# Quantised tiles as unsigned bytes centred by VectorE, and residual halves added ahead of the last accumulators

## The chip, the cores and the metric

The kernel runs on one core of a Trainium2 chip. The metric is the device time of one execution in microseconds (us), the median of several runs.

## The reference

`x` is (2, 512, 1024), `ctx` is (2, 1024, 1024), all float32. Four blocks follow each other, each on the layer norm of the running `x`, each added to it:

```python
def fake_quant(x, scale, zp):
    q = jnp.clip(jnp.round(x / s + z), 0.0, 255.0)
    return (q - z) * s
x = x + fake_quant(_layernorm(x)) @ fake_quant(ctx)                 # quantised product
x = x + _L0_ffn_ref(_layernorm(x), ...)     # four streams, mixed by a 50-step Sinkhorn normalisation
x = x + _L1_xattn_ref(_layernorm(x), ctx, Wq, bq, Wk, bk)           # softmax attention on ctx
x = x + _L1_ffn_ref(_layernorm(x), ...)     # out = (silu(gate) * up) @ down_w.T, each with a LoRA of rank 16
```

The change touches the first line and the very end of the last.

## The kernel before

The five engines have their own programs, written out by hand in order; semaphores join them, and each engine works strictly in its order. Tokens lie in 8 tiles of 128 rows (`g`), `ctx` in 16 tiles of 128 rows (`n`, 8 for each of the two batches).

**The front: quantisation.** SP's queue loads `x` tiles 0 to 3, context tiles 0 to 7, `x` tiles 4 to 7, context tiles 8 to 15 and then the sixteen tiles of Wq and Wk, each into the staging place `FSTAGE[n]` of a context tile once that tile has been taken (`front`, which waits on `q2_ok`). For an `x` tile VectorE forms the mean and the variance (L1532 to L1534), ScalarE a square root (L871), and VectorE the scale and the bias (`quant_rest`, L1521 to L1548). Then a tile, of `x` or of context, passes three engines:

```python
e.activation(st, st, ACT.Relu, bias=z2, scale=col(RQ2))                   # ScalarE, L887 (x: L880)
e.tensor_scalar(FSTAGE[n], FSTAGE[n], 255.0, MAGIC, ALU.min, ALU.add)     # VectorE, clip_q, L1560 (x: clip_x, L1556)
e.tensor_scalar(Q2[n // KP][:, n % KP, :], FSTAGE[n], 1.0, -(MAGIC + QHALF), ALU.mult, ALU.add)  # GpSimd, centre_q, L754 (x: centre_x, L749)
```

The division and the lower bound are ScalarE's; the upper bound and the rounding (adding 1.5 x 2^23 in float32) are VectorE's; GpSimd takes the constant off again together with 128 and writes bfloat16, on which TensorE works: it turns the `x` tile (L2506; ScalarE takes it out of PSUM, L894), sums the columns (L2525) and multiplies (L2560). VectorE adds the product to `x` (`add_product`, L1603). Between these ScalarE makes the upper halves of the weight tiles and scales the tiles (`weight_hi`, L931, L933), and GpSimd subtracts for the lower halves in four pieces a tile (`weight_lo`, L761), the last tile VectorE (L1721). TensorE's product of Wq and Wk needs all of them. Behind it run VectorE's Sinkhorn steps (L1685 to L1687) and TensorE's products (L2492 to L2494) side by side.

**The end: down projection.** A matrix product is done as seven products of blocks (names A11, A12, S1, S2, S4, S3, A22 in this order; `BLOCKS`), a scheme of Strassen's kind, and each float32 operand as two float16 halves, so three matmuls a pair (L2938). There are four output parts (`p`), each in three chunks (`j`, `SETS`) of 4, 4 and 3 pairs. The weights of chunk `j + 1` are prepared while TensorE works on chunk `j`: TensorE makes the LoRA factor product of a quarter (`down_fold`, L2872, into one PSUM bank), VectorE adds it to the loaded weights and frees the bank (`down_add`, L1975); four times in turn. Then VectorE forms the sums S1 to S4 (`form`, L1862), ScalarE copies the upper halves (L1129) and VectorE makes the lower ones (`block_lo`, L1867). In the first chunk of part `p + 1` VectorE also collects the seven accumulators of part `p` into four outputs: `scaled` (L1993) adds a bank, `added` (L1996) adds two tiles, and every one of the 13 steps raises `acc_v` by one. Two outputs get the residual by `residual_sum`; the two others as four additions of float16 halves, in `end_fourth` and `end_third`. TensorE's first products of a part wait on `acc_v` until their bank has been read (`down_product`), SP's `send` waits until an output is complete, and `load_sum` until the place of a residual is free.

Which product of chunk `j` each factor product follows is set in TensorE's last loop:

```python
first = 3 if j == HT else 2
for n, name in enumerate(BLOCKS):
    down_product(j, name)
    if j + 1 < HT + CHUNKS and first <= n < first + 4:
        down_fold(j + 1, n - first)
```

Of the kernel before, what the change touches and what calls it, by code (L numbers as in the profile page):

```python
# [6 lines left out]
B, S, D = 2, 512, 1024  # L7
# [3 lines left out]
BT = S // P  # L11
# [29 lines left out]
F32, F16, BF16 = mybir.dt.float32, mybir.dt.float16, mybir.dt.bfloat16  # L41
# [131 lines left out]
def build(nc, x, ctx, ctx_t, consts, small_w, w_branch, wq, wk, bqk, gate_w, up_w, tail_w,  # L173
          down_w, gate_a, gate_bt, up_a, up_bt, down_a, down_bt, out_t, x_keep, xt_keep, t_keep):
    stack = ExitStack()
    with stack:
# [156 lines left out]
        def factors_of(g, si, sj):  # L333
# [34 lines left out]
        v_step, scale_ok, gate_ok, bq_ok, var_ok, ln_ok, x_clip, q_clip = (  # L368
            sem(n) for n in ("v_step", "scale_ok", "gate_ok", "bq_ok", "var_ok", "ln_ok",
                             "x_clip", "q_clip"))  # L370
# [164 lines left out]
        def _(e):  # L535
# [80 lines left out]
            def load_sum(p, i):  # L616

                a_, b_ = ((0, 0), (0, 1), (1, 1), (1, 0))[i]
                if i >= 2:
                    e.wait_ge(sum_v, 2 * p + i - 1)  # L620
                elif p:
                    e.wait_ge(acc_v, ACCS * (p - 1) + (10, 12)[i])
                else:
                    e.wait_ge(t_lo, 3 * (HT // 2))
                    for n in range(2):
                        e.wait_ge(r_kept[n], LANDED + 16 * len(RESIDUAL))
                e.dma_start(residual(i), xt_keep[2 * p + a_, :, :, b_ * HALF:(b_ + 1) * HALF]).then_inc(res_in[i % 2], 16)

            def send(p):
                for (a_, b_), made in (((0, 0), 2), ((0, 1), 6), ((1, 1), 10), ((1, 0), ACCS)):  # L630
# [97 lines left out]
        def _(e):  # L728
# [16 lines left out]
            def centre_x(g):  # L745
                e.wait_ge(x_clip, g + 1)
                if g >= BT:
                    e.wait_ge(q1t_p, g - BT + 1)
                e.tensor_scalar(Q1[:, g % BT, :], XS[g % 2], 1.0, -(MAGIC + QHALF), ALU.mult,  # L749
                                ALU.add).then_inc(q1_ok, 1)  # L750
# [51 lines left out]

            centre_q(0)
            centre_x(0)
            centre_q(1)
            centre_q(2)
            centre_q(3)
            centre_x(1)
            centre_q(4)
            centre_q(5)  # L810
            centre_q(6)
            centre_q(7)
            centre_q(8)
            centre_q(9)
            centre_x(2)
            centre_q(10)
            centre_q(11)
            centre_q(12)
            weight_lo(0)
            weight_lo(1)  # L820
            centre_x(3)
            centre_q(13)
            centre_x(4)
            weight_lo(2)
            centre_x(5)
            centre_q(14)
            centre_q(15)
            weight_lo(3)
            centre_x(6)
            weight_lo(4)  # L830
            weight_lo(5)
            centre_x(7)
# [31 lines left out]
        def _(e):  # L864
# [11 lines left out]
            def quant_x(g):  # L876
# [3 lines left out]
                e.activation(XS[g % 2], X[:, g, :], ACT.Relu, bias=NMR[:, g:g + 1],  # L880
                             scale=RST[:, g:g + 1]).then_inc(x_relu, 1)

            def quant_ctx(n):
# [3 lines left out]
                e.activation(st, st, ACT.Relu, bias=z2, scale=col(RQ2)).then_inc(q_relu, 1)  # L887
# [619 lines left out]
        def _(e):  # L1507
# [521 lines left out]
            def take_seventh(p):  # L2029

                e.wait_ge(acc_v, ACCS * p + 4)
                scaled(p, out_part(1, 0), "S3", out_part(1, 0))
                e.wait_ge(acc_v, ACCS * p + 6)
                scaled(p, out_part(1, 1), "S3", out_part(1, 1))

            def end_fourth(p):
# [6 lines left out]
            def end_third(p):  # L2043

                e.wait_ge(res_in[1], LANDED + 16 * (2 * p + 2))
                for s_ in range(2):
# [1108 lines left out]
```

## Time and profile before

| what | value |
|---|---|
| median of 3 runs | 1146.93 us (1146.1 to 1147.59) |
| the profiled execution | 1146.65 us |
| its span | 1144.8 us |
| TensorE clock granted, mean | 0.984 of full speed |
| busy: TensorE, VectorE, ScalarE, GpSimd | 1081.6, 913.7, 523.7, 155.3 us |
| front, 0 to 108 us: TensorE, VectorE, ScalarE, GpSimd busy | 74.6, 99.1, 86.2, 70.1 us |
| end, 1020 to 1145 us: TensorE, VectorE busy | 116.6, 83.1 us |
| DMA | 118.44 MB, mean 103 GB/s |

The span runs from the first to the last instruction of the profiled execution; its own time holds a little besides. The matmuls' ends are modelled, so a TensorE that shows as busy need not be at its peak; matmuls of one kind follow each other faster than their single durations say.

### The profile page before, as it was taken

The page shows a single profiled execution, that of the slowest core. Times are in us where ns is not written, and L with a number is a line of the kernel's source. Part 1 is how long each engine was busy: PE and PEld are TensorE (multiplying, and loading weights), DVE is VectorE, ACT ScalarE, POOL GpSimd, SP SyncE. Part 2 cuts the span into 40 slices and gives each one's busy share as a digit, 9 for nine tenths or more (in the row PEclk, how much of TensorE's full clock was granted, in tenths as well). Part 3 has the DMA queues.
Part 4 walks back from the last instruction along what each step waited for, and adds up shares of the span by engine and source line. Part 5 has one row for each costly group of instructions (what it writes and reads, how often), then busy time and mean ns, then how long its engine had stood idle before and what let it go on. Part 6 is the DMA issues. An engine that isn't in the chain of part 4 may idle for free.

```text
span 1144.8 us, 16323 instructions
## 1 busy us (share of the span) xinstructions
PE 1081.6 (94%) x6028; PEld 532.2 (46%) x6034; DVE 913.7 (80%) x1830; ACT 523.7 (46%) x815; POOL 155.3 (14%) x183
## 2 busy tenths in 40 slices
PE   4787999899999999988999999999999999999998
PEld 2444554654444444433444444444444444444443
DVE  8998988889995267878888888888878786757675
ACT  6887752874145225654545354535353442222221
POOL 4875350064005010000000000000000000000000
PEclk9998999999999999998999999999999999999999
DMA  9720000114032017775154534252221273232221
GB/s 369 277 102 1 2 1 1 74 42 143 1 110 83 6 48 212 188 161 129 38 148 128 156 93 122 101 157 74 102 88 40 56 279 117 84 102 86 89 74 56
DMA packets 104208, 118.44 MB, mean 103 GB/s; under 512 B 74753, under 2 KB 78977, under 8 KB 104129
## 3 DMA queue, kind: packets, MB, share of 16 engines
q1 hardware_dynamic: 104128, 117.40, 33.3%
q8 instruction: 48, 0.79, 0.3%
q14 instruction: 32, 0.25, 0.1%
HBM read 86.97 MB, written 16.78 MB: 91 GB/s over the span
## 4 chain that ended last, share of the span: by engine, by line
PE 72%; DVE 19%; ACT 4%; issue 2%; DMA 1%; SPq 0%; DVEq 0%; ACTq 0%
PE PAIR L2840 32%; PE PAIR L2938 14%; PE PAIR L2492 6%; PE PAIR L2493 6%; PE PAIR L2494 6%; DVE X L1734 2%; PE PAIR L2795 2%; DVE T4B L1996 1%; DVE PAIR L1686 1%; DVE POOL L1560 1%; PE PAIR L2860 1%; DVE BST L1532 1%; DVE POOL L1867 1%; DVE X L1603 1%; PE PAIR L2872 1%
## 5 line engine op out<-in xcount | busy, mean ns | idle before, releaser
L2840 PE MATMUL PAIR<-XT,POOL 128*128 128x512 f16 x1008 | 232.9, 385 | 7.8 <-DMA XT<-POOL 4.0
L2840 PEld LDWEIGHTS PAIR<-XT,POOL 128*128 128x128 f16 x1008 | 98.7, 99 | 125.9 <-issue 14.0
L1129 ACT ACTIVATE POOL<-STG 128x512 f16<-128x512 f32 (+1 forms) x167 | 96.2, 612 | 74.6 <-DVE STG L1975 69.9
L2492 PE MATMUL PAIR<-POOL 128*128 128x512 f16 x336 | 127.9, 381 | 2.2 <-DVE POOL L1777 2.2
L2493 PE MATMUL PAIR<-POOL 128*128 128x512 f16 x336 | 127.9, 381 | 0.0
L2494 PE MATMUL PAIR<-POOL 128*128 128x512 f16 x336 | 127.7, 380 | 0.0
L2938 PE MATMUL PAIR<-POOL 128*128 128x512 f16 x528 | 117.9, 379 | 0.0
L2840 PE MATMUL PAIR<-X,POOL 128*128 128x512 f16 x504 | 115.7, 379 | 0.2 <-DMA X<-POOL 0.2
L1129 ACT ACTIVATE POOL<-ST 128x512 f16<-128x512 f32 (+1 forms) x64 | 39.5, 617 | 161.8 <-DVE ST L1862 161.8
L1867 DVE TENSOR_TENSOR POOL<-STG,POOL 128x512 f16<-128x512 f32 (+1 forms) x167 | 106.4, 669 | 1.1 <-ACT POOL L1129 1.1
L801 POOL MEMSET STG<- 96x1024 f32 (+1 forms) x12 | 11.0, 923 | 522.6 <-DVE POOL L1867 475.9
L2938 PEld LDWEIGHTS PAIR<-POOL 128*128 128x128 f16 x528 | 51.1, 98 | 59.5
L1975 DVE SCALAR_TENSOR_TENSOR STG<-STG,PAIR 128x512 f32<-128x512 f32 (+1 forms) x48 | 30.8, 641 | 58.6 <-PE PAIR L2872 58.3
L2840 PEld LDWEIGHTS PAIR<-X,POOL 128*128 128x128 f16 x504 | 48.3, 98 | 55.7 <-issue 1.1
L2840 PE MATMUL PAIR<-T4B,POOL 128*128 128x512 f16 x252 | 57.8, 379 | 1.2 <-issue 1.2
L1847 DVE SCALAR_TENSOR_TENSOR STG<-STG,PAIR 128x1024 f32<-128x1024 f32 x43 | 52.1, 1214 | 0.0
L2494 PEld LDWEIGHTS PAIR<-POOL 128*128 128x128 f16 x336 | 32.9, 98 | 40.3 <-issue 1.0
L1686 DVE RECIPROCAL PAIR<-LORA 128x16 f32<-128x16 f32 (+1 forms) x168 | 46.8, 279 | 5.8
L2492 PE MATMUL PAIR<-XT,POOL 128*128 128x512 f16 x128 | 48.5, 379 | 1.2 <-ACT XT L1039 1.2
L2494 PE MATMUL PAIR<-XT,POOL 128*128 128x512 f16 x128 | 48.5, 379 | 0.0
L2493 PE MATMUL PAIR<-XT,POOL 128*128 128x512 f16 x128 | 48.5, 379 | 0.0
L2492 PEld LDWEIGHTS PAIR<-POOL 128*128 128x128 f16 x336 | 32.8, 97 | 32.7 <-DVE POOL L1777 4.3
(342 smaller groups left out, 1944.1 us busy)
## 6 DMA issues: line engine op xcount, KB each, us to landing
STG<-in_gate_w SPq DMA_DIRECT2D x21, 512.0 KB, 5.0
STG<-in_up_w SPq DMA_DIRECT2D x21, 512.0 KB, 5.8
STG<-in_ctx_t SPq DMA_DIRECT2D x16, 512.0 KB, 3.8
STG<-in_ctx SPq DMA_DIRECT2D x16, 512.0 KB, 4.2
STG<-in_down_w SPq DMA_DIRECT2D x16, 512.0 KB, 4.4
POOL<-in_ctx SPq DMA_DIRECT2D x12, 512.0 KB, 10.8
X<-in_x SPq DMA_DIRECT2D x8, 512.0 KB, 9.4
xt_keep<-POOL SPq DMA_DIRECT2D x16, 256.0 KB, 3.0
```

Of the source, the lines that this page charges most:

```text
L1129: e.activation(block(j, name)[:, 0, :, :], src, ACT.Copy).then_inc(b_hi, 1)
L1686: chain(e.reciprocal(rr, rs))
L1734: i = e.scalar_tensor_tensor(xs, H[:, g, sj * CST:(sj + 1) * CST], factors_of(g, si, sj), xs, ALU.mult, ALU.add)
L1847: e.scalar_tensor_tensor(st, st, WS, PAIR[aux.pair("fold", n)][:, :], ALU.mult, ALU.add).then_inc(s_add, 1)
L1867: e.tensor_tensor(blk[:, 1, :, :], block_source(j, name)[0], blk[:, 0, :, :], ALU.subtract).then_inc(b_lo, 1)
L1975: e.scalar_tensor_tensor(st, st, WS, bank_f[:, 0:depth(j) * P], ALU.mult, ALU.add).then_inc(s_add, 1)
L2492: e.matmul(dst, l_hi, r_hi, start=first, stop=False)
L2493: e.matmul(dst, l_hi, r_lo, start=False, stop=False)
L2494: return e.matmul(dst, l_lo, r_hi, start=False, stop=last)
L2795: i = e.matmul(PAIR[pr][:, k * P + c0:k * P + c0 + w], fa[0:GRP * 32, k * P:(k + 1) * P], fb[0:GRP * 32, j * P:j * P + w], start=True, sto ...
L2840: i = e.matmul(dst, blk[:, a_, k, :], src[:, b_, k, :], start=(opens and k == 0 and n == 0), stop=(k == KD // 2 - 1 and n == 2), skip_grou ...
L2938: last = e.matmul(dst, blk[:, a_, i - i0, :], src[:, b_, :], start=first, stop=(c == NSET - 1 and i == i1 - 1 and n == 2))
```

## The change

1. ScalarE writes its result as unsigned bytes into the first quarter of the same place, which rounds and bounds it. VectorE's clips and GpSimd's centring passes go; at the clips' places in VectorE's order stand centring passes that read the bytes, subtract 128 and write bfloat16. Wait for wait they follow ScalarE's counter and raise the counters that GpSimd's raised; `centre_x` takes over the wait on `q1t_p`.
2. In the down projection the four additions of residual halves move: two ahead of `take_third`, two ahead of `take_seventh`; `take_fourth` (formerly the end of `end_third`) follows `take_seventh`. The numbers in the waits on `acc_v` follow. In the first chunk of each part the factor products of the next chunk come one product later.

```diff
-            def centre_q(n):
-                e.wait_ge(q_clip, n + 1)
-                e.tensor_scalar(Q2[n // KP][:, n % KP, :], FSTAGE[n], 1.0, -(MAGIC + QHALF), ALU.mult,
-                                ALU.add).then_inc(q2_ok, 1)
...
-            centre_q(0)
-            centre_x(0)
...
             weight_lo(0)
             weight_lo(1)
-            centre_x(3)
...
-                e.activation(XS[g % 2], X[:, g, :], ACT.Relu, bias=NMR[:, g:g + 1],
+                e.activation(XS[g % 2].bitcast(U8)[:, 0:D], X[:, g, :], ACT.Relu, bias=NMR[:, g:g + 1],
                              scale=RST[:, g:g + 1]).then_inc(x_relu, 1)
...
-                e.activation(st, st, ACT.Relu, bias=z2, scale=col(RQ2)).then_inc(q_relu, 1)
+                e.activation(st.bitcast(U8)[:, 0:D], st, ACT.Relu, bias=z2, scale=col(RQ2)).then_inc(q_relu, 1)
...
-            def clip_x(g):
+            def centre_x(g):
                 e.wait_ge(x_relu, g + 1)
-                e.tensor_scalar(XS[g % 2], XS[g % 2], 255.0, MAGIC, ALU.min, ALU.add).then_inc(x_clip, 1)
-
-            def clip_q(n):
+                if g >= BT:
+                    e.wait_ge(q1t_p, g - BT + 1)
+                e.tensor_scalar(Q1[:, g % BT, :], XS[g % 2].bitcast(U8)[:, 0:D], 1.0, -QHALF, ALU.mult,
+                                ALU.add).then_inc(q1_ok, 1)
+
+            def centre_q(n):
                 e.wait_ge(q_relu, n + 1)
-                e.tensor_scalar(FSTAGE[n], FSTAGE[n], 255.0, MAGIC, ALU.min, ALU.add).then_inc(q_clip, 1)
+                e.tensor_scalar(Q2[n // KP][:, n % KP, :], FSTAGE[n].bitcast(U8)[:, 0:D], 1.0, -QHALF, ALU.mult,
+                                ALU.add).then_inc(q2_ok, 1)
...
             def end_second(p):
-                e.wait_ge(acc_v, ACCS * p + 5)
+                e.wait_ge(acc_v, ACCS * p + 7)
                 added(out_part(0, 1), out_part(1, 1))
...
+            def third_residual(p):
+                e.wait_ge(res_in[1], LANDED + 16 * (2 * p + 2))
+                for s_ in range(2):
+                    e.wait_ge(acc_v, ACCS * p + 4 + s_)
+                    added(out_part(1, 0), residual(3)[:, s_, :])
...
+            def take_seventh(p):
+                e.wait_ge(acc_v, ACCS * p + 10)
+                scaled(p, out_part(1, 0), "S3", out_part(1, 0))
+                scaled(p, out_part(1, 1), "S3", out_part(1, 1))
...
                 if last:
+                    third_residual(p)
                     take_third(p)
...
                 if last:
+                    fourth_residual(p)
                     take_seventh(p)
+                    take_fourth(p)
                 block_lo(j, "S3")
                 block_lo(j, "A22")
-                if last:
-                    end_fourth(p)
-                    end_third(p)
...
                 elif name == "S4":
                     if p and c == 0:
-                        e.wait_ge(acc_v, at + 5)
+                        e.wait_ge(acc_v, at + 7)
...
                 elif name == "S3":
                     if p and c == 0:
-                        e.wait_ge(acc_v, at + 8)
+                        e.wait_ge(acc_v, at + 12)
...
-                first = 3 if j == HT else 2
+                first = 3 if (j - HT) % NSET == 0 else 2
```

`fourth_residual` is `end_fourth` under another name, and `take_fourth` the last line of `end_third`. `send` waits for 8 and 12 in place of 6 and 10 with two of its four outputs.

GpSimd's order at the start of the weights, before (L754 and L749 are the centring passes, L761 a quarter of a weight subtraction):

```order
L754 TENSOR_SCALAR POOL<-POOL 128x1024 [waits q_clip] x2
L754 TENSOR_SCALAR POOL<-XT 128x1024 [waits q_clip]
L761 TENSOR_TENSOR POOL<-POOL 128x256 [waits w_hi]
L761 TENSOR_TENSOR POOL<-POOL 128x256 x3
L761 TENSOR_TENSOR POOL<-POOL 128x256 [waits w_hi]
L761 TENSOR_TENSOR POOL<-POOL 128x256 x3
L749 TENSOR_SCALAR POOL<-POOL 128x1024 [waits x_clip]
L754 TENSOR_SCALAR POOL<-XT 128x1024 [waits q_clip]
L749 TENSOR_SCALAR POOL<-POOL 128x1024 [waits q1t_p,x_clip]
L761 TENSOR_TENSOR POOL<-POOL 128x256 [waits w_hi]
```

and of the change, from the last of the constants on (L748 is now the subtraction):

```order
L741 AFFINE_SELECT NEGM<-NEGM 128x128 [waits p_step]
L748 TENSOR_TENSOR POOL<-POOL 128x256 [waits w_hi]
L748 TENSOR_TENSOR POOL<-POOL 128x256 x3
L748 TENSOR_TENSOR POOL<-POOL 128x256 [waits w_hi]
L748 TENSOR_TENSOR POOL<-POOL 128x256 x3
```

Nothing stands ahead of or between the weight subtractions any more.

TensorE's order in the first chunk of the last part, before (L2938 the products, by their banks PAIR0 to PAIR3 in the order of `BLOCKS`; L2872 the factor products), from S1 on:

```order
L2938 MATMUL PAIR<-POOL 128x512 [waits acc_v,b_lo]
L2938 MATMUL PAIR<-POOL 128x512 x11
L2872 MATMUL PAIR<-LORA 128x128 [waits s_add]
L2872 MATMUL PAIR<-LORA 128x128 x3
L2938 MATMUL PAIR<-X,POOL 128x512 [waits acc_v,b_lo]
L2938 MATMUL PAIR<-X,POOL 128x512 x11
L2872 MATMUL PAIR<-LORA 128x128 [waits s_add]
L2872 MATMUL PAIR<-LORA 128x128 x3
```

and of the change (L2908 and L2842 are the same two lines):

```order
L2908 MATMUL PAIR<-POOL 128x512 [waits acc_v,b_lo]
L2908 MATMUL PAIR<-POOL 128x512 x11
L2908 MATMUL PAIR<-X,POOL 128x512 [waits acc_v,b_lo]
L2908 MATMUL PAIR<-X,POOL 128x512 x11
L2842 MATMUL PAIR<-LORA 128x128 [waits s_add]
L2842 MATMUL PAIR<-LORA 128x128 x3
L2908 MATMUL PAIR<-POOL 128x512 [waits acc_v,b_lo]
L2908 MATMUL PAIR<-POOL 128x512 x11
L2842 MATMUL PAIR<-LORA 128x128 [waits s_add]
L2842 MATMUL PAIR<-LORA 128x128 x3
```

The first factor product has moved from behind S1 to behind S2, and each of the others by one product.

VectorE's order in the same chunk, before (L1867 `block_lo`, L1993 `scaled`, L1996 `added`, L1975 `down_add`):

```order
L1867 TENSOR_TENSOR POOL<-STG,POOL 128x512 [waits b_hi]
L1993 SCALAR_TENSOR_TENSOR T4B<-PAIR,T4B 128x512 [waits mul_p,acc_v] x2
L1867 TENSOR_TENSOR POOL<-STG,POOL 128x512 [waits b_hi] x2
L1996 TENSOR_TENSOR T4B<-T4B,LORA 128x512 [waits acc_v,front_in14]
L1996 TENSOR_TENSOR T4B<-T4B,LORA 128x512 [waits acc_v]
L1996 TENSOR_TENSOR T4B<-T4B,LORA 128x512 [waits acc_v,front_in15]
L1996 TENSOR_TENSOR T4B<-T4B,LORA 128x512 [waits acc_v]
L1993 SCALAR_TENSOR_TENSOR T4B<-PAIR,T4B 128x512 [waits mul_p,acc_v]
L1975 SCALAR_TENSOR_TENSOR STG<-STG,PAIR 128x512 [waits fold_p,stg_in3] x2
```

and of the change, the same stretch:

```order
L1834 TENSOR_TENSOR POOL<-STG,POOL 128x512 [waits b_hi]
L1963 TENSOR_TENSOR T4B<-T4B,LORA 128x512 [waits acc_v,front_in14]
L1963 TENSOR_TENSOR T4B<-T4B,LORA 128x512 [waits acc_v]
L1960 SCALAR_TENSOR_TENSOR T4B<-PAIR,T4B 128x512 [waits mul_p,acc_v]
L1960 SCALAR_TENSOR_TENSOR T4B<-PAIR,T4B 128x512 [waits mul_p]
L1960 SCALAR_TENSOR_TENSOR T4B<-PAIR,T4B 128x512 [waits mul_p,acc_v]
L1834 TENSOR_TENSOR POOL<-STG,POOL 128x512 [waits b_hi] x2
L1942 SCALAR_TENSOR_TENSOR STG<-STG,PAIR 128x512 [waits fold_p,stg_in3] x2
```

The other two residual additions stand four rows further up; as many instructions as before precede the down add.

## Rows read from the trace of the kernel before

**Rows 1.** The page, busy tenths of VectorE in 40 slices of the span.

```profile
DVE  8998988889995267878888888888878786757675
```

**Rows 2.** The chain of waits, 10 to 106 us: shares by line.

```profile
by line: DVE POOL L1560 11.6%; DVE X L1603 10.4%; DVE XT L1597 8.4%; DVE BST L1532 8.0%; DVE BST L1533 7.5%; DMA POOL<-in_ctx 6.7%; DVE POOL L1556 5.6%; DVE XT L1560 4.2%; issue 3.7%; PE PAIR L2560 3.3%; DVE SM L1523 2.8%; DVE SM L1534 2.8%
```

**Rows 3.** Table by stretch: busy us (instructions) by engine, clock, DMA share, GB/s.

```profile
10.00:37.00 27.00, 19.46 (x82) 9.40 (x84) 25.74 (x52) 24.59 (x24) 15.85 (x13) 0.94 1.03 409
37.00:92.00 55.00, 43.11 (x390) 25.53 (x393) 52.30 (x83) 47.05 (x53) 46.97 (x64) 0.97 0.37 136
```

The engines are PE, PEld, DVE, ACT and POOL, in this order.

**Rows 4.** Timeline of VectorE in the front: start us, us, instruction.

```profile
17.55 0.84 DVE L1581 SCALAR_TENSOR_TENSOR SM<-SM 128x1 f32<-128x1 f32 x1
...
19.41 0.16 DVE L1522 TENSOR_TENSOR SM<-SM 128x3 f32<-128x3 f32 x1
...
20.54 0.23 DVE L1548 TENSOR_SCALAR SM<-SM,CST_ 128x3 f32<-128x3 f32 x1
...
36.36 1.29 DVE L1560 TENSOR_SCALAR POOL<-POOL 128x1024 f32<-128x1024 f32 x2
...
40.39 0.62 DVE L1522 TENSOR_TENSOR SM<-SM 128x2 f32<-128x2 f32 x1
...
55.97 0.77 DVE L1522 TENSOR_TENSOR SM<-SM 128x2 f32<-128x2 f32 x1
...
59.76 0.53 DVE L1548 TENSOR_SCALAR SM<-SM,CST_ 128x2 f32<-128x2 f32 x1
...
104.22 1.22 DVE L1721 SCALAR_TENSOR_TENSOR XT<-STG,XT 128x1024 f16<-128x1024 f32 x1
```

**Rows 5.** Timeline of GpSimd, the first two weight tiles.

```profile
40.97 5.51 POOL L761 TENSOR_TENSOR POOL<-POOL 128x256 f16<-128x256 f32 x8
```

**Rows 6.** Twelve of the sixteen context clips: ns min/median/max, first and last start.

```profile
L1560 DVE TENSOR_SCALAR POOL<-POOL x12: 685/694/1532, 11.5 to 37.0; 128x1024 f32<-128x1024 f32 x12
```

**Rows 7.** Timeline of VectorE: corrections from PSUM; a scaling to 2 bytes.

```profile
93.72 2.35 DVE L1597 SCALAR_TENSOR_TENSOR XT<-PAIR,XT 128x1024 f16<-128x1024 f32 x2 [0.29 <-DVE SM L2098]
...
432.09 0.68 DVE L1837 TENSOR_SCALAR LORA<-STG 96x1024 f16<-96x1024 f32 x1
```

**Rows 8.** ScalarE's waits, 37 to 92 us: us in total, times, longest.

```profile
ACT POOL L880 <- DVE SM L1548: 4.9, 2, 3.5
```

**Rows 9.** ScalarE's first weight copy; the last four context loads and all landings.

```profile
37.05 1.05 ACT L931 ACTIVATE POOL<-POOL 128x1024 f16<-128x1024 f32 x1
...
L552 SPq DMA_DIRECT2D XT<-in_ctx x4: 435/1080/2982, 15.1 to 17.8; - x4
...
DMA to landing us min/median/max: 6.5/13.8/17.4
```

**Rows 10.** TensorE's waits from 900 us on; its timeline at one boundary.

```profile
PE PAIR L2872 <- DVE STG L1975: 3.8, 3, 1.3
...
1044.28 0.40 PE L2872 MATMUL PAIR<-LORA 96*128 96x128 f16 x4 [1.28 <-DVE STG L1975]
...
1047.11 0.39 PE L2872 MATMUL PAIR<-LORA 96*128 96x128 f16 x4
...
1049.93 0.39 PE L2872 MATMUL PAIR<-LORA 96*128 96x128 f16 x4
```

**Rows 11.** Timeline of VectorE at the same boundary.

```profile
1043.55 0.68 DVE L1975 SCALAR_TENSOR_TENSOR STG<-STG,PAIR 128x512 f32<-128x512 f32 x1
...
1051.76 0.69 DVE L1867 TENSOR_TENSOR POOL<-STG,POOL 128x512 f16<-128x512 f32 x1
```

**Rows 12.** Timeline of VectorE at the very end.

```profile
1133.41 1.42 DVE L1993 SCALAR_TENSOR_TENSOR T4B<-PAIR,T4B 128x512 f32<-128x512 f32 x2 [2.40 <-PE PAIR L2938]
...
1137.30 1.29 DVE L1993 SCALAR_TENSOR_TENSOR T4B<-PAIR,T4B 128x512 f32<-128x512 f32 x2 [0.52 <-PE PAIR L2938]
1138.69 2.94 DVE L1996 TENSOR_TENSOR T4B<-T4B,LORA 128x512 f32<-128x512 f32 x4
1141.66 0.69 DVE L1993 SCALAR_TENSOR_TENSOR T4B<-PAIR,T4B 128x512 f32<-128x512 f32 x1
```

More of the change, by code:

```diff
@@ L621, in load_sum @@
                 elif p:
-                    e.wait_ge(acc_v, ACCS * (p - 1) + (10, 12)[i])
+                    e.wait_ge(acc_v, ACCS * (p - 1) + (10, 6)[i])
                 else:
@@ L629, in send @@
             def send(p):
-                for (a_, b_), made in (((0, 0), 2), ((0, 1), 6), ((1, 1), 10), ((1, 0), ACCS)):
+                for (a_, b_), made in (((0, 0), 2), ((0, 1), 8), ((1, 1), 12), ((1, 0), ACCS)):
                     m = 2 * p + a_
@@ L2041, in end_fourth, with take_fourth @@
                     added(out_part(1, 1), residual(2)[:, s_, :])
-            def end_third(p):
-                e.wait_ge(res_in[1], LANDED + 16 * (2 * p + 2))
-                for s_ in range(2):
-                    e.wait_ge(acc_v, ACCS * p + 10 + s_)
-                    added(out_part(1, 0), residual(3)[:, s_, :])
+            def take_seventh(p):
+                e.wait_ge(acc_v, ACCS * p + 10)
+                scaled(p, out_part(1, 0), "S3", out_part(1, 0))
+                scaled(p, out_part(1, 1), "S3", out_part(1, 1))
+            def take_fourth(p):
                 e.wait_ge(acc_v, ACCS * p + 12)
@@ L2106, in _ @@
             quant_rest(0, 1)
-            clip_q(0)
+            centre_q(0)
             loaded_stats(3)
             norm_ask(1, 4)
-            clip_x(0)
-            clip_q(1)
-            clip_q(2)
+            centre_x(0)
+            centre_q(1)
+            centre_q(2)
             zero_point_parts()
             quant_rest(1, 4)
-            clip_q(3)
+            centre_q(3)
             loaded_stats(4)
-            clip_x(1)
-            clip_q(4)
-            clip_q(5)
-            clip_q(6)
-            clip_q(7)
+            centre_x(1)
+            centre_q(4)
+            centre_q(5)
+            centre_q(6)
+            centre_q(7)
             loaded_stats(5)
-            clip_q(8)
+            centre_q(8)
             loaded_stats(6)
-            clip_q(9)
+            centre_q(9)
             column_parts(0)
-            clip_x(2)
+            centre_x(2)
             add_product(0)
             norm_ask(4, 6)
-            clip_q(10)
-            clip_q(11)
-            clip_q(12)
+            centre_q(10)
+            centre_q(11)
+            centre_q(12)
             add_product(1)
             quant_rest(4, 6)
-            clip_q(13)
+            centre_q(13)
             second_lo(0)
-            clip_q(14)
-            clip_x(3)
+            centre_q(14)
+            centre_x(3)
             second_lo(1)
-            clip_x(4)
+            centre_x(4)
             add_product(2)
-            clip_x(5)
+            centre_x(5)
             loaded_stats(7)
-            clip_q(15)
+            centre_q(15)
             norm_ask(6, 8)
@@ L2481, in _ @@
             take_fifth(p)
+            third_residual(p)
             take_third(p)
             end_second(p)
+            fourth_residual(p)
             take_seventh(p)
-            end_fourth(p)
-            end_third(p)
+            take_fourth(p)
         @prog.tensor
```

45 lines of the change are left out of this document (6 added, 39 removed).

## Prediction

> **What bounds the kernel now.** The page's forty slices come first: in the first four (0 to 114 us) VectorE shows eights and nines [rows 1]. So I asked for the chain of waits from 10 to 106 us. It is VectorE nearly throughout: 11.6% + 5.6% + 4.2% of 96 us, 20.5 us, are the 24 clips (L1560, L1556) [rows 2]. The table by stretch agrees: VectorE is busy 25.7 of 27 us, then 52.3 of 55 [rows 3]. The stretch ends with VectorE's last weight correction at 104.2 us [rows 4], for which TensorE's next product waits. From there VectorE's normalisation steps and TensorE's products run side by side to about 197 us, so what is won before moves everything behind it. Later TensorE sets the pace. In the down projection it waits for VectorE three times, 3.8 us in all, each time with a factor product (L2872) [rows 10], and at the very end VectorE alone has over 3 us left [rows 12].
>
> **The quantisation.** Removed: 24 clips on VectorE and 24 centring passes on GpSimd. Added: 24 centring passes on VectorE, from bytes to bf16. The rest keeps its place on each engine, and the loads wait for q2_ok as before.
>
> A clip alone takes 0.69 us and the next instruction starts 0.60 behind it (two take 1.29 [rows 4]); the longest takes 1.53 [rows 6]. In the chain the mean is 20.5 / 24 = 0.85 us. The difference is GpSimd: while it works clips stretch, and so do operations on two or three numbers. The correction step of a norm takes 0.62 us while GpSimd subtracts weights and 0.16 us while it does not [rows 4, 5].
>
> The new pass is unknown, since no byte operand stands in the trace. Bounds: 0.60 us if it runs as the clip does; 1.13 us at one element per cycle, the spacing of two 1024-wide corrections that read PSUM (2.35 us for two, the second 1.2 long) [rows 7]. The nearest row is a TENSOR_SCALAR with a 4-byte source and a 2-byte result, 96x1024, at 0.68 us [rows 7]: unequal sizes do not cost the fast rate. I take 0.60 and keep 1.13.
>
> The Trainium skill, Vector Engine (DVE) Microarchitecture Reference, section 5.1, lets a one-source operation take two elements per cycle whenever source and result lie in SBUF and their outer dimension is even; 2-byte types are asked for in the packed modes alone. By that rule the pass costs 0.60 us and the sum is the one below. No run so far shows it for bytes.
>
> VectorE's account: 24 x 0.60 = 14.4 in place of 20.5, **-6.1 us**. The norm terms of tiles 6 and 7 take 4.3 us beside GpSimd (55.97 to 60.29), the same chain 1.4 us when GpSimd is idle (19.41 to 20.77) [rows 4]; with the centring passes gone from its queue GpSimd will have done by then all the weights it was given, **-2.9 us**. The zero-point parts were held twice, one of them 0.84 us in place of 0.16 [rows 4], **-1.4 us**. The norm terms of tiles 4 and 5, from 40.4 us, stay held: there weight subtractions block [rows 5], and these stay. Together -10.4 us on VectorE.
>
> Not all of it arrives; late next is **ScalarE**. Between 37 and 92 us it works 47.05 of 55 us [rows 3] and waits 7.9, most of it for the quantisation terms and roots of VectorE (4.9 us for L1548 alone) [rows 8]. Its first weight copy starts at 37.05 and cannot come much sooner: the last context tiles are issued up to 17.8 us and land up to 17.4 us later, at 35.2 [rows 9]; the first weight tile is queued behind them, 0.52 MB at 409 GB/s [rows 3], at 36.5. So ScalarE yields at most 0.5 + 7.9 = 8.4 us. Following both engines' orders with these durations, I find ScalarE almost without a gap from 36.5 us on, and VectorE waiting 1 to 1.5 us each for two context tiles and for the root of tiles 4 and 5. I take **-7.7 us**; bounds in this case -5 and -8.4. GpSimd's own part is free: its weight subtractions (5.5 us for two tiles [rows 5]) start when ScalarE delivers.
>
> The Trainium skill, SBUF — State Buffer, says that the second port pair is locked for a whole instruction, by GpSimd or by a VectorE operation that uses two ports. That speaks against the change, since the byte passes want that pair as the clips did and will meet the weight subtractions; the trace agrees (0.62 against 0.16 us), and it is why nothing is won at 40 us above.
>
> **The down projection.** The four residual halves move ahead; nothing is added. At a boundary VectorE has 21 instructions in one unbroken row, from 1030.58 on; the last is the first down add of the next chunk, at 1043.55 [rows 11]. TensorE's second factor product waits for it and starts at 1044.28, 1.28 us late [rows 10]. As many instructions as before stand ahead of that add, so it still ends at 1044.2. But each factor product moves behind one more product of 12 matmuls, which with a factor product takes 2.82 us (1047.11 to 1049.93 [rows 10]): the first comes at 1042.6, the second at 1045.5, behind the add. The wait goes, three times: **-3.8 us**. What that endangers: the fourth factor product now comes right ahead of the next chunk. From its start at 1049.93 to the end of block A12's correction (1051.76 + 0.69) are 2.5 us [rows 10, 11]; TensorE wants the block after 2.8. Slack 0.3 us, so nothing lost. TensorE's changed waits on acc_v: the seventh count (S4) is reached near 1034.5 and wanted at 1042.6, the twelfth (S3) near 1041.7, wanted at 1045.5; both free. Block corrections now stand behind the residual adds' wait for their loads, but these are issued before the last chunk's products. SP's sends of a boundary end 1.3 us sooner.
>
> At the very end VectorE takes S2 and S1 from 1133.41, waits twice for TensorE, 0.52 us each, and has seven operations from S3 on, to 1142.35 [rows 12]. Now eleven follow from 1133.41 without a gap: 1.42 + 1.46 + 0.65 + 0.73 + 1.46 + 1.30 + 0.72 = 7.74, to 1141.15, 1.2 us sooner. The last two sends are then only 0.7 us apart and I leave 0.1 for that: **-1.1 us**.
>
> **Sum.** -7.7 - 3.8 - 1.1 = -12.6. The profiled execution took 1146.65 us (span 1144.8): 1134.05. The median of the three runs lies 0.28 above it: **1134.3 us**.
>
> **Rivals.**
> 1. GpSimd goes on blocking. Weight subtractions fall on the norm terms of tiles 6 and 7, and the 2.9 us stay. For it: the row at 40.39, where subtractions alone block. Against: ScalarE has given no weight in the 3 us before. -7.7 becomes -4.8: 1137.2 us. Chance 0.13.
> 2. Bytes at one element per cycle: 24 x 0.53 = 12.7 us more on VectorE than forecast, against 10.4 won. The quantisation is 0 to 2.3 us slower, the rest stands: about 1143 us. For it: no row has a byte operand. Against: rows 7. Chance 0.10.
> 3. Block A12 or S1 is missed at each boundary: the 3.8 us go and up to 0.5 each is added, 1138 to 1139.6 us. For it: the slack of 0.3. Chance 0.05.
> 4. **Slower.** The byte passes run at one element per cycle and wait for GpSimd's port besides, so that each costs what the longest clip does, 1.53 us [rows 6]: 24 x (1.53 - 0.85) = +16.3, less 4.3 for the small operations and 4.9 at the back, +7.1: 1154 us. It decides from a mean of 1.33 us on (24 x 0.48 - 9.2 = 2.3). Against: whoever takes one element per cycle need not wait for the other port, as the corrections of rows 7 show. Chance 0.03.
>
> **Numbers.** Forecast 0.69, with 1132 to 1137 of its own. A measurement of this kernel can tell about 0.2%, 2.3 us. Rivals 1 to 3 are faster too, but for the slow end of the second: faster 0.93, same 0.04, slower 0.03. The range, 1131.5 to 1141, leaves out rivals 2 and 4 and a gain past ScalarE's bound.
>
> **What would show it.** A byte pass of 0.69 us with starts 0.60 apart; no TENSOR_SCALAR on GpSimd; ScalarE's waits between 36 and 84 us under 2 us; the last weight correction near 96.5 us; no wait of TensorE with its factor products; 7.7 us from S2's sum to the last one. A byte pass near 1.2 us, or ScalarE still waiting some 8 us, makes the first term wrong; a wait of TensorE at A12 or S1 the second.

## The result, and the profile after

| what | before | after |
|---|---|---|
| median | 1147.26 us (6 runs, 1146.1 to 1148.96) | 1137.01 us (6 runs, 1134.49 to 1141.28) |
| the profiled execution | 1146.65 us | 1135.42 us |
| its span | 1144.8 us | 1133.6 us |
| busy: TensorE, VectorE, ScalarE, GpSimd | 1081.6, 913.7, 523.7, 155.3 us | 1079.0, 904.4, 523.5, 128.4 us |

The ratio is 0.9914, 95% interval 0.9892 to 0.9935: faster by 10 us. The profiled pair differs by 11.2 us. A second set of six runs of the changed kernel gave 0.990 (0.9876 to 0.9925), told below.

The forty slices of VectorE, for [rows 1] (28.3 us each): in the front it is still nearly full, the first slice a seven and no longer an eight.

```profile
DVE  7998889889994267978888888888887886767676
```

The table by stretch, for [rows 3] (PE, PEld, DVE, ACT, POOL busy, clock, DMA share, GB/s): GpSimd does nothing between 10 and 37 us, VectorE has 3.3 us less there. ScalarE now works 50.8 of 55 us between 37 and 92, where it worked 47.05.

```profile
10.00:37.00 27.00, 20.30 (x97) 10.30 (x96) 22.40 (x54) 25.02 (x25) 0.00 (x0) 1.00 1.03 409
37.00:92.00 55.00, 46.37 (x480) 28.57 (x481) 51.72 (x95) 50.84 (x59) 40.86 (x60) 0.92 0.35 136
```

The new pass, all sixteen context tiles (ns min/median/max, first and last start, forms), for [rows 6]: 0.69 us, from one byte a number to two.

```profile
L1526 DVE TENSOR_SCALAR POOL<-POOL x12: 685/687/695, 11.5 to 35.0; 128x1024 bf16<-128x1024 uint8 x12
L1526 DVE TENSOR_SCALAR POOL<-XT x4: 689/692/908, 35.6 to 51.1; 128x1024 bf16<-128x1024 uint8 x4
```

The timeline of VectorE in the front, for [rows 4] (start us, us, instruction):

```profile
39.58 0.59 DVE L1486 TENSOR_TENSOR SM<-SM 128x2 f32<-128x2 f32 x1
...
43.60 0.91 DVE L1526 TENSOR_SCALAR POOL<-XT 128x1024 bf16<-128x1024 uint8 x1
44.43 1.16 DVE L1521 TENSOR_SCALAR POOL<-POOL 128x1024 bf16<-128x1024 uint8 x1
...
46.64 1.17 DVE L1521 TENSOR_SCALAR POOL<-POOL 128x1024 bf16<-128x1024 uint8 x1
...
53.27 0.16 DVE L1486 TENSOR_TENSOR SM<-SM 128x2 f32<-128x2 f32 x1
...
82.48 0.77 DVE L1500 TENSOR_SCALAR SM<-SM 128x4 f32<-128x4 f32 x1
...
98.21 1.22 DVE L1688 SCALAR_TENSOR_TENSOR XT<-STG,XT 128x1024 f16<-128x1024 f32 x1
```

Norm terms of tiles 6 and 7 run free (0.16 us a step at 53.27), those of tiles 4 and 5 are still held for four of their six steps (0.59 us at 39.58), and four byte passes, the fourth at 64.21, take 0.9 to 1.17 us. The last weight correction comes at 98.21 us instead of 104.22: **6.0 us sooner**.

ScalarE's waits from 37 to 92 us, for [rows 8] (us in total, times, longest): what stood at 4.9 us, the wait for the quantisation terms (now L1511), is 0.9.

```profile
ACT SM L834 <- DVE SM L1500: 1.2, 1, 1.2
ACT POOL L894 <- DMA POOL<-in_wq: 1.1, 1, 1.1
ACT POOL L843 <- DVE SM L1511: 0.9, 1, 0.9
```

TensorE at the second boundary, for [rows 10]: the second factor product (1038.20) has no wait in its row, nor has any from 900 us on.

```profile
1035.39 0.39 PE L2842 MATMUL PAIR<-LORA 96*128 96x128 f16 x4
1035.61 2.75 PE L2908 MATMUL PAIR<-POOL 128*128 128x512 f16 x12
1038.20 0.39 PE L2842 MATMUL PAIR<-LORA 96*128 96x128 f16 x4
```

From the first factor product of one such boundary to that of the next were 53.81 us (986.22 to 1040.03) and are 52.36 (983.03 to 1035.39): 1.45 us less, more than the 1.28 of the wait's row. The rows above hold the rest: in an unbroken row an instruction starts ahead of the recorded end of the one before it (1038.20 against 1035.61 + 2.75 = 1038.36), and the row of a wait counts from that recorded end, so that the step costs 1.28 + 0.16 = 1.44 us.

VectorE at the very end, for [rows 12]: 7.85 us from the first start to the last end, without a gap in between, where it was 8.94.

```profile
1123.28 1.42 DVE L1960 SCALAR_TENSOR_TENSOR T4B<-PAIR,T4B 128x512 f32<-128x512 f32 x2 [2.40 <-PE PAIR L2908]
...
1129.11 2.02 DVE L1960 SCALAR_TENSOR_TENSOR T4B<-PAIR,T4B 128x512 f32<-128x512 f32 x3
```

So the profiled 11.2 us are: 6.0 at the end of the front, of which 5.8 are left at 930 us (the same VectorE instruction at 930.38 and 924.60); 3 x 1.45 = 4.35 at the boundaries; 1.1 at the end.

### The profile page after: what moved, and what is told of

Read it like the earlier page. It is cut to its first block, busy times and chain, and to the rows that moved or that the text cites. A ratio compares the mean times of both kernels' runs of the same rounds, so it can differ in the third digit from the quotient of the medians.

```text
span 1133.6 us, 16301 instructions
## 1 busy us (share of the span) xinstructions
PE 1079.0 (95%) x6034; PEld 532.3 (47%) x6034; DVE 904.4 (80%) x1830; ACT 523.5 (46%) x815; POOL 128.4 (11%) x159
## 4 chain that ended last, share of the span: by engine, by line
PE 76%; DVE 14%; ACT 4%; DMA 3%; issue 2%; SPq 1%; DVEq 0%; ACTq 0%
PE PAIR L2810 33%; PE PAIR L2908 17%; PE PAIR L2462 7%; PE PAIR L2463 6%; PE PAIR L2464 6%; DVE X L1701 2%; PE PAIR L2765 2%; DMA POOL<-in_wq 1%; DMA X<-in_x 1%; DVE PAIR L1653 1%; PE PAIR L2830 1%; PE PAIR L2842 1%; DVE LORA L1652 1%; DVE LORA L1654 1%; PE PAIR L2669 1%
## 5 line engine op out<-in xcount | busy, mean ns | idle before, releaser
L2908 PE MATMUL PAIR<-POOL 128*128 128x512 f16 x528 | 117.9, 379 | 0.0
L2908 PEld LDWEIGHTS PAIR<-POOL 128*128 128x128 f16 x528 | 51.0, 98 | 58.8
```

The lines of the kernel that those rows point to most:

```text
L2908: last = e.matmul(dst, blk[:, a_, i - i0, :], src[:, b_, :], start=first, stop=(c == NSET - 1 and i == i1 - 1 and n == 2))
```

## The experiments: the two halves

The first kernels take the change apart. They were timed in one set with 22 runs of before on the same chip. Those 22 fall into two groups some 4 us apart, half in each (more on this below), so the medians here can't settle differences of 1 us; the traces do.

**The front alone.** The quantisation's part of the diff, nothing else.

```diff
-                e.activation(st, st, ACT.Relu, bias=z2, scale=col(RQ2)).then_inc(q_relu, 1)
+                e.activation(st.bitcast(U8)[:, 0:D], st, ACT.Relu, bias=z2, scale=col(RQ2)).then_inc(q_relu, 1)
...
-                e.tensor_scalar(FSTAGE[n], FSTAGE[n], 255.0, MAGIC, ALU.min, ALU.add).then_inc(q_clip, 1)
+                e.tensor_scalar(Q2[n // KP][:, n % KP, :], FSTAGE[n].bitcast(U8)[:, 0:D], 1.0, -QHALF, ALU.mult,
+                                ALU.add).then_inc(q2_ok, 1)
```

> The kernel before with the quantisation's part of the change alone (bytes from ScalarE, centring on VectorE, none on GpSimd); the down projection stays as it was. Theory: the two halves of the change are independent, and this one carries what the trace of the changed kernel shows at 104 us (last weight correction 6.0 us earlier): 5.8 to 6.0 us less than before, ratio 0.995, three waits of TensorE of 1.27 us at the boundaries as before. Rival (the front's gain is larger and part of it is eaten behind it, by a loss that comes with the new down projection): 7.7 us less.

Measured: 1141.43 us (1138.99 to 1146.45), beside 1148.33 for before, ratio 0.994 (0.9917 to 0.9964), 6.9 us where 5.8 to 6.0 were forecast; the three waits of TensorE are there (3.8 us). The profiled execution was the slowest, 1146.45 us, and shows why in one row (VectorE's timeline, start, us):

```profile
82.16 0.21 DVE L1497 BATCH_NORM_AGGREGATE SM<-BST 128x2 f32<-128x12 f32 x1
82.40 8.30 DVE L1500 TENSOR_SCALAR SM<-SM 128x4 f32<-128x4 f32 x1
90.73 0.20 DVE L1576 RECIPROCAL SM<-SM 128x8 f32<-128x8 f32 x1
```

and, from GpSimd's timeline of the same execution:

```profile
83.09 2.57 POOL L748 TENSOR_TENSOR XT<-XT 128x256 f16<-128x256 f32 x4
85.61 5.07 POOL L748 TENSOR_TENSOR XT<-STG,XT 128x256 f16<-128x256 f32 x8
```

An addition on four numbers a row takes 8.30 us instead of 0.77, and ends at 90.70, just where GpSimd's last twelve subtractions end (85.61 + 5.07 = 90.68). Ahead of it this execution agrees with the changed kernel's within 0.1 us. Behind it it is 5 us later: an operation that before has at 93.08 us comes at 92.22 here and at 87.05 there. Neither profile of before nor of the changed kernel shows this long hold.

**The down projection alone.**

```diff
                 if last:
+                    third_residual(p)
                     take_third(p)
...
-                first = 3 if j == HT else 2
+                first = 3 if (j - HT) % NSET == 0 else 2
```

> The kernel before with the down projection's part of the change alone (residual halves earlier, factor products one product later); the quantisation stays. Theory from the two traces: each boundary, from its first factor product to that of the next, took 53.81 us and takes 52.36, 1.45 less and not the 1.27 of the wait; three times 4.35, and 1.1 at the very end, together 5.4 us less than before, ratio 0.9953. Rival (the waits' own 3.8 us are all there is, and 0.5 of the difference comes from something else): 4.9 us.

Measured: 1143.49 us beside 1148.33, ratio 0.9947 (0.9927 to 0.9967). Its profile has the long hold as well (8.32 us at 88.28), so it is read behind 930 us, where it stands 3.95 us late: at S2's sum it is 0.41 early, 4.36 us won, and from there to the end another 1.1. That is 5.45 us, as the two traces said (the medians: 4.8).

**One edit each of the two.** First the factor products alone:

```diff
-                first = 3 if j == HT else 2
+                first = 3 if (j - HT) % NSET == 0 else 2
```

> The kernel before with one edit: the factor products of the next chunk come one product later in the first chunk of each part. VectorE's order is untouched. Theory: this edit alone removes the three waits, since VectorE's first down add still ends near 1044.2 us of before's time and the second factor product then comes near 1045.5: 4.3 us less than before, the very end unchanged at 8.9 us from S2's sum to the last. Rival (the residual halves must be out of the way first): a wait of over 0.5 us stays at each boundary and the gain is under 3 us.

Measured: 1144.58 us, ratio 0.9959 (0.9944 to 0.9974). No wait of TensorE from 930 us on; 0.67 us late at 930 and 3.68 early at S2's sum, 4.35 us; the end takes 8.94 us as before.

Then the residual halves alone, with the waits on `acc_v` that go with them:

> The kernel before with the residual halves moved and the waits that follow from it, but the factor products where they were. Theory: as many instructions of VectorE as before stand ahead of the first down add, so the three waits of 1.27 us stay, and only the very end is shorter: 1.1 us less than before. Rival (the residual halves were what held the down add): 4 us or more less than before, and no waits.

Measured: 1146.0 us (1142.72 to 1151.84), ratio 0.9985 (0.9967 to 1.0003), which by itself shows nothing. The profile does: the waits stay (its list of waits, against [rows 10]):

```profile
PE PAIR L2875 <- DVE STG L1975: 3.6, 3, 1.2
```

and the end takes 1133.40 to 1141.25, 7.85 us. So the factor products' place gives the 4.35 us and needs nothing of the residual halves; these give the 1.1 and nothing at the boundaries. By the traces the two halves of the change add up: 5.8 and 5.45 us for 11.2.

## The experiments: the long hold and the port

The unexpected row needed an answer, since it could move the median by as much as a term of the sum.

**The changed kernel again.**

> The changed kernel again, to see how its executions spread. In the kernels with one half of the change, one addition of VectorE on four numbers a row (the variance's epsilon ahead of the last norm's root, near 82 or 88 us) took 8.3 us where it takes 0.77 in the changed kernel and in the kernel before: GpSimd's subtractions ran in an unbroken row for all of that time. Theory (a lottery at this place, in both kernels): the executions fall into two groups about 5 us apart, near 1135.5 and 1141 us, and so do those of before, near 1146.5 and 1150.5; the ratio of the medians stays near 0.991. Rival (one slow execution, nothing more): the times lie round 1135.5 within 2 us.

Measured: 1134.9 us, ratio 0.990 (0.9876 to 0.9925). Five executions lie between 1133.64 and 1136.22, one at 1141.49, and neither profile of the changed kernel has the long hold (0.77 and 0.76 us). With the six of the first set: nine of twelve between 1133.6 and 1137.7, three between 1140.8 and 1141.5. Before has such groups as well: in the set of the halves, on one chip, eleven executions between 1145.5 and 1147.8 and eleven between 1148.9 and 1151.6; in the two later sets 4 of 14 and 5 of 11 are in the upper group. That all upper ones have the hold is not shown. Two profiled executions can be laid beside one with the same front and no hold: at 135 us the front's half is 5.1 us behind the changed kernel, the down projection's half 4.7 us behind before.

The hold is not the only source of the spread. Profiles without it drift apart between 200 and 260 us, where no edit reaches. Against the changed kernel's first profile the one with the pause (next) loses 3 us there and the one with floats gains 1.6. The table of that stretch for the changed kernel and for the one with the pause, with TensorE's granted clock at 0.97 and 0.94 (with floats 1.00); why was not followed:

```profile
200.00:260.00 60.00, 54.11 (x359) 35.27 (x357) 52.59 (x168) 42.45 (x72) 27.54 (x24) 0.97 0.28 90
200.00:260.00 60.00, 54.11 (x357) 35.87 (x356) 49.67 (x168) 44.11 (x76) 24.87 (x23) 0.94 0.24 79
```

**A pause for GpSimd** ahead of the row that did it:

```diff
+            e.wait_ge(var_ok, 7)
             weight_lo(12)
             weight_lo(13)
```

> The changed kernel with one wait on GpSimd: ahead of the subtraction of weight tile 12 it waits until VectorE has written the input of the last root (var_ok at 7). GpSimd is then idle for about 1 us where VectorE has its small additions, and ends some 1 us later than at 90.9, which nobody waits for before 95 us. Theory (an operation of VectorE that needs the port pair waits until GpSimd's row breaks): the addition never takes more than about 1 us, the group near 1141 us is gone, all executions lie between 1133.5 and 1137.5 and the median is 1135. Rival (the spread has another source): same spread and median as the changed kernel of this call.

Measured: 1135.01 us (1133.55 to 1137.49, 5 runs), ratio 0.9889 (0.987 to 0.9909). The wait shows on GpSimd (its timeline) and moves VectorE's last weight correction by 0.2 us, from 98.21 to 98.45:

```profile
83.91 2.60 POOL L748 TENSOR_TENSOR XT<-XT 128x256 f16<-128x256 f32 x4 [0.75 <-DVE SM L1579]
```

The addition took 0.78 us, as it does without the pause in an execution that is not held. None of five executions, nor of four of a later kernel with the same wait, is above 1140 us (one of the four took 1139.22; its profile has no hold and loses 3.0 us between 200 and 260 us). At three in twelve, nine without one would come about by chance 7 or 8 times in 100. But five executions of the kernel with floats (below), without a pause, are not above 1140 us either; with them among the unpaused it is three in seventeen, and 17 times in 100. So that the pause cures the hold is not shown. The median is that of the changed kernel.

**GpSimd's first tiles later.**

```diff
+            e.wait_ge(ln_ok, 8)
             weight_lo(0)
             weight_lo(1)
```

> The changed kernel with one wait on GpSimd: its first subtraction waits until VectorE has written the scale and bias of tiles 6 and 7 (ln_ok at 8, 54.9 us). Its work of 3 tiles from 38.9 to 50.1 us moves behind that, so that no subtraction runs beside the norm terms of tiles 4 and 5 (2.8 us for 1.4) and the byte passes at 43.6, 44.4 and 46.6 us (0.91, 1.16, 1.17 us for 0.69). Both theories: these take 1.4 us and 0.69 each, VectorE is 2.5 us ahead at 54 us. Theory of short holds (each operation waits for the piece of 0.64 us that is under way): the lead stays, the time falls by 1 to 2.5 us. Theory of the unbroken row (an operation waits until GpSimd's row breaks): GpSimd now has some 25 us of subtractions in one row from 54 us on, and a byte pass or a small addition in it is held for many microseconds: a hold of over 3 us appears between 55 and 80 us, and the time is 3 to 15 us longer.

Measured: 1143.67 us (1139.69 to 1145.78, 9 runs), ratio 0.9961 (0.9947 to 0.9976). Half of each theory. The norm terms of tiles 4 and 5 and the passes up to 52 us run free, as both said. The lead, 1.55 us at 40.3, is gone by 52 us in waits for ScalarE, and ScalarE then waits 4.6 us for GpSimd, whose eight tiles from 55.33 us form one row of 21.2 us:

```profile
ACT POOL L895 <- POOL POOL L748: 4.6, 1, 4.6
```

In that long row no operation of VectorE is held past 1.04 us, against the theory of the unbroken row. Yet at 87.75 the same addition as above takes 7.04 us and again ends with GpSimd's last subtraction (89.71 + 5.06 = 94.77). So an unbroken row on GpSimd is not enough for a long hold. The kernel is 5.3 us behind the changed one when this addition starts and 8.6 at the last weight correction, so most of the loss is older than the hold.

**The pieces.** Each weight tile in eight pieces of 128 columns, then in two of 512, in place of four of 256:

```diff
-                for q in range(0, D, CST):
-                    qs = slice(q, q + CST)
+                for q in range(0, D, CST // 2):
+                    qs = slice(q, q + CST // 2)
```

(for 512 columns `2 * CST` in both places)

> The changed kernel with GpSimd's subtraction of a weight tile in eight pieces of 128 columns in place of four of 256. Theory (an operation of VectorE that wants the port pair waits for the end of the piece under way, and now and then for the end of the row): a hold is at most about 0.4 us long in place of 0.64, so the passes at 43.6, 44.4, 46.6 and 64 us take under 1.05 us, the small operations near 0.4, and VectorE's last weight correction comes 1 to 2 us earlier than at 98.2, if a tile still takes GpSimd under 3.2 us; time 1 to 2 us below the changed kernel. Rival (a piece has a fixed part of some 0.2 us): a tile takes 3.5 us or more, ScalarE and TensorE wait for GpSimd's halves, and the time is the same or up to 4 us longer.

> The same in two pieces of 512 columns. Theory of the piece: holds are up to 1.3 us each; the held passes take 1.3 to 1.9 us, the small operations beside a subtraction about 1 us, VectorE ends the front 3 to 6 us later than in the changed kernel and the time is 2 to 6 us longer. Rival (VectorE gets the port between GpSimd's accesses, the hold is a fixed 0.5 us whatever the piece): holds as before, time the same within 1 us.

Measured: 1143.8 us (1142.1 to 1144.99, 0.9961) with 128 columns, 1138.03 us (1137.82 to 1138.91, 0.9914) with 512. The timeline of VectorE with the small pieces:

```profile
42.60 0.75 DVE L1526 TENSOR_SCALAR POOL<-XT 128x1024 bf16<-128x1024 uint8 x1
43.27 0.91 DVE L1521 TENSOR_SCALAR POOL<-POOL 128x1024 bf16<-128x1024 uint8 x1
...
71.09 3.26 DVE L1500 TENSOR_SCALAR SM<-SM 128x4 f32<-128x4 f32 x1
...
84.28 9.43 DVE L1500 TENSOR_SCALAR SM<-SM 128x4 f32<-128x4 f32 x1
```

from GpSimd's, the same kernel:

```profile
61.47 12.86 POOL L748 TENSOR_TENSOR POOL<-POOL 128x128 f16<-128x128 f32 x32 [0.58 <-ACT POOL L896]
...
88.93 6.23 POOL L748 TENSOR_TENSOR XT<-STG,XT 128x128 f16<-128x128 f32 x16
```

and VectorE's with the large ones:

```profile
39.05 0.93 DVE L1485 TENSOR_TENSOR SM<-SM 128x2 f32<-128x2 f32 x1
40.01 1.08 DVE L1486 TENSOR_TENSOR SM<-SM 128x2 f32<-128x2 f32 x1
...
44.32 1.65 DVE L1521 TENSOR_SCALAR POOL<-POOL 128x1024 bf16<-128x1024 uint8 x1
...
74.80 1.13 DVE L1500 TENSOR_SCALAR SM<-SM 128x4 f32<-128x4 f32 x1
...
85.01 0.17 DVE L1500 TENSOR_SCALAR SM<-SM 128x4 f32<-128x4 f32 x1
```

The short hold grows with the piece under way: the same x pass (44.43 us in the changed kernel) takes 0.91, 1.16 and 1.65 us with 128, 256 and 512 columns. With small pieces VectorE is 1.6 us ahead at 46.1 us, as expected. The addition stands ahead of two roots, near 73 and 82 us in the changed kernel (0.61 and 0.77 us there). With small pieces both are held, the first for 3.26 us to the end of a row of GpSimd (61.47 + 12.86 = 74.33), the second for 9.43 us, to 93.71, inside GpSimd's last 16 pieces (88.93 to 95.16). All six executions take over 1142 us: my forecast of 1 to 2 us faster was wrong. With large pieces the two take 1.13 and 0.17 us, no hold passes 1.7 us, the executions lie within 1.1 us of each other, and the short holds cost 3.1 us at the last weight correction (101.35), as forecast. The median is 1.0 and 3.1 us above the two of the changed kernel, which were taken in other sets.

The Trainium skill, SBUF — State Buffer, section "Who interferes with whom", has whichever issues first keep the shared pair for the whole instruction. If the one that waits comes next, which the page does not say in so many words, no hold passes one piece, 0.64 us here. The trace agrees for the passes; the holds of 7 to 9.4 us, over eleven and more pieces, do not fit.

## The experiments: what bounds the front now

**Floats in place of bytes.** ScalarE leaves float32, VectorE's pass reads it; the rounding and the upper bound are left out.

```diff
-                e.activation(st.bitcast(U8)[:, 0:D], st, ACT.Relu, bias=z2, scale=col(RQ2)).then_inc(q_relu, 1)
+                e.activation(st, st, ACT.Relu, bias=z2, scale=col(RQ2)).then_inc(q_relu, 1)
```

> The changed kernel with float32 in place of bytes: ScalarE writes 4 bytes a number into the same place, VectorE's centring pass reads them and writes bfloat16. The rounding and the upper bound are left out. Theory (the gain is one pass less on VectorE and none on GpSimd; the byte type costs and gives nothing): a pass is 0.69 us with starts 0.60 apart as for bytes, ScalarE's 1.23 us stay, and the time is the changed kernel's within 1 us. Rival (a source of one byte runs faster or slower than one of four): the pass differs by over 0.1 us, 24 passes by over 2.4 us.

```profile
L1526 DVE TENSOR_SCALAR POOL<-POOL x12: 685/688/696, 11.6 to 35.4; 128x1024 bf16<-128x1024 f32 x12
```

Measured: 1134.2 us, ratio 0.9881 (0.9863 to 0.990), beside 1134.9 for the changed kernel. 688 ns against 687: four bytes or one make no difference to the pass. So the gain is the pass that is gone, and the byte is what allows it: the changed kernel has no other instruction that rounds or bounds above, which ScalarE's write as bytes takes over.

**Bytes, but centred by GpSimd**, in its order of before; VectorE has neither clip nor pass.

```diff
...
             weight_lo(1)
+            centre_x(3)
+            centre_q(13)
+            centre_x(4)
             weight_lo(2)
...
```

> The changed kernel with its 24 centring passes given back to GpSimd, in its order of before, now reading bytes; VectorE has neither clip nor pass. Theory (VectorE's length is what counts): VectorE is relieved of 16.4 us, the front goes by ScalarE, whose waits of 2.5 us between 37 and 86 us go; 1 to 2.5 us faster than the changed kernel. Rival (what counts is GpSimd's hold on the port and its own length): GpSimd works some 65 us of the 80 before 90 us, norm terms of tiles 6 and 7 are held again (4.3 us for 1.8), ScalarE waits for them and for centred tiles, and the time is 1 to 4 us longer than the changed kernel's.

Measured: 1135.23 us (1134.67 to 1138.87), ratio 0.9896 (0.988 to 0.9913), the changed kernel's time. VectorE has 17.9 us of waits from 8 to 98 us where the changed kernel has 5.3; the largest (us in total, times, longest):

```profile
DVE LORA L1562 <- ACT LORA L897: 6.4, 2, 6.0
DVE X L1594 <- PE PAIR L2538: 4.5, 3, 2.0
DVE XT L1588 <- ACT XT L914: 4.3, 3, 1.9
```

ScalarE, which waits only 1.8 us between its first weight copy and 86 us, reaches its copy of the seventh transposed tile at 85.08 us, the changed kernel at 85.80. Neither forecast came: relieving VectorE further gives nothing, and GpSimd's 24 passes harm nothing. That it gives nothing because ScalarE has no more to give is argued from these waits, not shown: the profiled execution has the long hold too (7.06 us at 83.04), so its end of the front can't be compared.

**ScalarE relieved.** With the pause, and two swaps in ScalarE's order:

```diff
-            quant_x(6)
-            q1_transposed(5)
             weight_hi(4)
+            quant_x(6)
+            q1_transposed(5)
...
-            norm_root(0, 4)
             weight_hi(9)
+            norm_root(0, 4)
```

> The kernel with the pause, and in ScalarE's order two swaps: the ninth weight tile's copies ahead of the root of tiles 0 to 3 (ScalarE waited 1.15 us there), and the fourth's ahead of the bytes of x tile 6 (0.87 us). Theory of my prediction (ScalarE is late next): its 2.0 us of waits go, the time falls by 1 to 2 us. Rival (VectorE, which waits only 1.8 us between 36 and 98 us, is the bound still): ScalarE is up to 2 us ahead at 85 us, GpSimd ends earlier, but VectorE's last weight correction moves by less than 0.7 us and so does the time.

Measured: 1136.22 us (1135.68 to 1139.22, 4 runs), ratio 0.9895 (0.9878 to 0.9912): no gain of 1 to 2 us. The seventh tile's copy is at 84.36, 1.4 us sooner, and VectorE's last weight correction at 99.27, 1.1 us later. ScalarE's lead is lost on VectorE, whose small operations stand between the two, beside GpSimd's last tiles; the pause had become 3.3 us long here, since GpSimd was early too, and put these tiles 1.7 us later than in the changed kernel. So this kernel shows that ScalarE alone does not set the end, not what the swaps would bring without the pause.

Between 36 us and the front's end VectorE waits 1.8 us and ScalarE, from its first copy to 86 us, 2.4: both are full to within 2 or 3 us. No version beats the changed kernel's median by a measurable amount.

## Why the prediction was right, and where it was not

The forecast was 1134.3 us, range 1131.5 to 1141; the profiled execution took 1135.42, the medians were 1137.0 and 1134.9. Of the 2.7 us to the first median the terms below make 1.4. The rest is the spread: that median lies 1.6 above its profiled execution, where the forecast had added 0.3 for before's.

- **The new pass** is 0.69 us with starts 0.60 apart, as taken, and not 1.13. The rule quoted from the Trainium skill (Vector Engine (DVE) Microarchitecture Reference, section 5.1) holds for a one-byte source in this trace.
- **VectorE's account, -10.4 forecast.** Adding up the starts' spacings without idle time from 8 us to the last weight correction gives 94.05 us before and 84.74 now: -9.3. The 24 passes fell from 21.0 to 16.4, -4.6 in place of -6.1. Here is the term that was mis-sized: "24 x 0.60 = 14.4" gave the passes no hold, though the next paragraphs said they want the port and keep meeting the subtractions. Four were held, 1.6 us in all beyond their spacing of 0.60. The norm terms of tiles 6 and 7 went from 4.3 to 1.8 us (-2.5 for -2.9, the last one held, 0.68), the zero-point parts from 2.8 to 1.3 (-1.5 for -1.4). Those of tiles 4 and 5, forecast to stay, gave 0.9 us, since two of their six steps run free.
- **What arrives, -7.7 forecast, -6.0 measured.** VectorE's idle time in that stretch rose by 3.3 us (1.98 to 5.28) where I had left 2.7. ScalarE was not "almost without a gap": its first copy is at 36.77 and not 36.5, and it waits 2.4 us between that and 86 us, where under 2 was to show the term; the last weight correction came at 98.21 and not near 96.5. Taking ScalarE for late next was half right. Relieving VectorE further brought nothing (bytes centred by GpSimd), but freeing ScalarE brought nothing either (the two swaps): the small operations beside GpSimd's last tiles come behind it. 0.2 of the 6.0 us are gone by 930 us; how was not followed.
- **Rival 1** (GpSimd goes on blocking tiles 6 and 7) did not come. What no row showed was the hold of 7 to 9 us on one addition. The kernel with the down projection's half alone, whose front is that of before, has it too, and the kernel with the front's half has it with the new front, so it can fall on both sides of the ratio. Two of the changed kernel's first six executions are in the upper group and one of the second six, beside medians of 1137.0 and 1134.9.
- **The boundaries, -3.8 forecast, -4.35 measured.** The mechanism was right and the term mis-sized: a wait of 1.28 us in the row cost 1.45 us from boundary to boundary, the overlap of 0.16 us with the instruction before it included. Rival 3 did not come: A12's correction begins at 1045.67 us, S1 finds its operands.
- **The end, -1.1**, is -1.1 (7.85 us for 7.74, from 8.94).
- **The sum.** -7.7 - 3.8 - 1.1 = -12.6 against -6.0 + 0.2 - 4.35 - 1.1 = -11.2. The front's miss of 1.7, and the 0.2 lost behind it, were partly hidden by the 0.55 at the boundaries: that much of the sum's closeness is luck.

## What to carry to other kernels

Let the engine that already touches a tile round and bound it in its own output type; the pass saved is the gain, and on which engine the rest of the work lands mattered little here once two engines were full. When passes move onto an engine that another one can hold up, give them the mean duration of their neighbours beside that other engine, not the free one. And look at single executions of a kernel whose times fall into groups: one row of a few numbers with several microseconds in it can move a median by as much as a change does.

## What the runs showed of the hardware that I had not expected

- VectorE's one-source addition on 128x4 numbers (L1500, L1537 in before, ahead of a norm's root) was held 3.3, 7.0, 7.1, 8.3, 8.3 and 9.4 us in five kernels' profiles, five times of six until GpSimd's row of subtractions ended. In the same rows other operations of VectorE, a byte pass among them (0.91 us at 62.70 with small pieces), were let in after one piece, and in the changed kernel's profile so was this one (0.77 us). Why it is passed over in some executions is open.
- GpSimd's subtraction of 128 rows takes 2.28, 2.57 and 3.13 us a tile in 2, 4 and 8 pieces: about 0.14 us fixed for each piece.
- ScalarE writes 128x1024 bytes in the time of floats (both 1.23 us), and the clip's two operations need no instruction any more.
- A gap of 1.28 us in TensorE's row of matmuls cost 1.45 us, three of them 4.35 (the changed kernel, the down projection's half and the factor products alone against before): the overlap of matmuls that follow each other is lost with the gap.
